# Slots without loops, GpSimd's row sums ahead of its transfers, and ScalarE's copies ahead of tests, in a graph attention and feed-forward kernel

## The reference

```python
def gnn(input1, input2, adj, a1, a2):          # input1 = layernorm(x)
    e = input1 @ a1 + (input2 @ a2).T          # 4096 x 4096
    e = where(e > 0, e, 0.2 * e)
    att = softmax(where(adj > 0, e, -9e15), axis=1)
    att = 0.1 * att * sum(adj, axis=1) + 0.9 * adj
    return att @ input2
x = x + gnn(layernorm(x), input2, adj, a1, a2)
x = x + layernorm(x) @ weight.T + bias
```

## Time and profile before

| | |
|---|---|
| median of 3 runs | 408.13 us (406.33 to 408.9) |
| profiled execution, own time | 405.57 us |
| its span, first to last instruction | 403.7 us |
| mean granted TensorE clock | 0.989 |
| PE, DVE, ACT, POOL busy | 91%, 77%, 62%, 38% |

### The profile page before, as it was taken

One profiled execution on the slowest core, in us unless ns is written; L12 is line 12 of the kernel. 1 busy time (PEld: TensorE's weight loads), 2 busy tenths in 40 slices (PEclk: granted clock), 3 DMA queues, 4 the chain that ended last, 5 costly groups with the idle time before them and its releaser, 6 DMA issues.

```text
span 403.7 us, 9169 instructions
## 1 busy us (share of the span) xinstructions
PE 368.8 (91%) x3237; PEld 319.9 (79%) x3237; DVE 311.4 (77%) x790; ACT 251.2 (62%) x638; POOL 152.0 (38%) x255
## 2 busy tenths in 40 slices
PE   0579999879999999999999599999999999999992
PEld 0368878678888888888888488888888888888881
DVE  3989788899796886959595764968869595968873
ACT  2499998787676492919376094764929293765100
POOL 1787051735353624243353503536341331500101
PEclk9999999999999999999999899999999999999997
DMA  6999996938565629091835608357290000000000
GB/s 208 253 213 215 219 180 117 202 69 182 110 141 108 140 60 190 29 190 48 154 82 119 134 15 164 71 103 145 55 196 26 15 15 2 13 3 15 13 2 29
DMA packets 17358, 42.84 MB, mean 106 GB/s; under 512 B 1936, under 2 KB 8608, under 8 KB 17312
## 3 DMA queue, kind: packets, MB, share of 16 engines
q0 software_dynamic: 9216, 33.56, 43.1%
q1 hardware_dynamic: 8096, 8.67, 6.8%
HBM read 73.66 MB, written 2.11 MB: 188 GB/s over the span
## 4 chain that ended last, share of the span: by engine, by line
PE 76%; ACT 11%; DVE 6%; issue 3%; DMA 2%; POOL 1%; SPq 0%; POOLq 0%; DVEq 0%; ACTq 0%
PE acc_u L598 25%; PE acc_v L598 25%; PE acc_y L598 22%; ACT steep L453 6%; ACT minus L506 2%; PE small L592 2%; DMA plus<-in 2%; PE small L578 1%; DVE plus L879 1%; DVE plus L756 1%; ACT weights_u L492 1%; PE turned L567 1%; ACT weights_v L498 1%; DVE minus L759 1%; POOL adj_all L339 0%
## 5 line engine op out<-in xcount | busy, mean ns | idle before, releaser
L453 ACT ACTIVATE steep<-s_bc,steep_s 128x256 bf16<-128x256 f32 x512 | 208.0, 496 | 11.5 <-DVE plus L756 11.4
L598 PE MATMUL acc_u<-weights_u,plus 128*128 128x258 f16 x1024 | 122.1, 275 | 5.6 <-issue 4.2
L598 PE MATMUL acc_y<-weights_y,adj_all 128*128 128x258 f16 x1024 | 121.1, 275 | 3.0 <-DVE lin L777 2.5
L598 PE MATMUL acc_v<-weights_v,minus 128*128 128x258 f16 x1024 | 120.3, 273 | 0.0
L598 PEld LDWEIGHTS acc_u<-weights_u,plus 128*128 128x128 bf16 x1024 | 100.3, 98 | 22.0 <-issue 4.8
L598 PEld LDWEIGHTS acc_y<-weights_y,adj_all 128*128 128x128 bf16 x1024 | 100.2, 98 | 18.7 <-DVE lin L777 2.8
L598 PEld LDWEIGHTS acc_v<-weights_v,minus 128*128 128x128 bf16 x1024 | 99.9, 98 | 14.4
L466 ACT ACTIVATE num<-acc_u,ac 128x129 f32<-128x129 f32 x32 | 11.5, 363 | 113.7 <-PE acc_u L598 113.7
L759 DVE TENSOR_TENSOR minus<-adj_all,plus 128x2048 bf16<-128x2048 bf16 x64 | 78.4, 1225 | 2.2
L756 DVE TENSOR_TENSOR plus<-adj_all,steep 128x2048 bf16<-128x2048 bf16 x64 | 78.5, 1226 | 0.9 <-ACT steep L453 0.9
L339 POOL DMA_DIRECT2D adj_all<-adj x64 | 36.0, 580 | 106.0 <-DVE minus L759 97.4
(11 more groups left out here) (78 smaller groups left out, 242.3 us busy)
## 6 DMA issues: line engine op xcount, KB each, us to landing
adj_all<-adj POOLq DMA_DIRECT2D x64, 512.0 KB, 8.9
plus<-in SPq DMA_DIRECT2D x4, 512.0 KB, 7.2
x_pre<-x SPq DMA_DIRECT2D x16, 128.0 KB, 2.1
x_res<-x SPq DMA_DIRECT2D x16, 128.0 KB, 2.2
out<-late SPq DMA_DIRECT2D x16, 128.0 KB, 5.2
s_rows<-s_bc SPq DMA_DIRECT2D x16, 1.0 KB
steep<-a SPq DMA_DIRECT2D x1, 64.0 KB, 3.1
a_bc<-a SPq DMA_DIRECT2D x1, 64.0 KB, 5.0
```

The costliest lines, as they stand in the source:

```text
L453: ins = nc.scalar.activation(steep[:, h, k, :], s1_bc[b][:, :], ACT.Relu, bias=steep_s2[:, jt:jt + 1], scale=STEEP)
L598: ins = nc.tensor.matmul(acc[:, 0:2 * WC], left[:, jt, cols(t)], right[:, jt, :, :].rearrange("p a b -> p (a b)"), start=(jt == 0), stop=( ...
```

## The change

Three things. First, `run_slots` no longer makes a loop: all 16 slots are written out on ACT, PE and DVE, and with n always a plain number the waits' values are constants. Second, POOL's slot has a new order. Third, ACT's two copies become a step that stands in a list: in slot 1 they are before quarters 2 and 3 of the tests, in the other slots at the end as they were.

```diff
-        def run_slots(eng, slot):
-            for c in range(BUFS):
-                slot(c, c)
-            with eng.Fori(1, CHUNKS // BUFS - 1) as quad:
-                for k in range(BUFS):
-                    slot(BUFS * quad + k, k)
-            for c in range(CHUNKS - BUFS, CHUNKS):
+        def run_slots(slot):
+            for c in range(CHUNKS):
                 slot(c, c % BUFS)
         def landed(n, b):
-            return 16 * (n // 2 + 1) if isinstance(n, int) else 8 * (n - b) + 16
+            return 16 * (n // 2 + 1)
...
             for c in range(CHUNKS):
                 b = c % 2
+                if c >= 1:
+                    post(c - 1, 1 - b)
+                if c + 2 < CHUNKS:
+                    row_sums(c + 2, b)
                 if c + BUFS < CHUNKS:
                     pool.wait_ge(y_done, 2 * c + 2)
                     pool.wait_ge(minus_ready, 4 * c + 4)
                     load_adj(c + BUFS)
-                if c >= 1:
-                    post(c - 1, 1 - b)
                 if c + 2 < CHUNKS:
-                    row_sums(c + 2, b)
                     factors(c + 2, b, False)
...
-                order = [0, 1, "first", "second", 2, 3] if isinstance(c, int) and c < 2 else \
-                    [0, 1, "first", 2, 3, "second"]
+                order = [0, 1, "first", "second", 2, 3, "copies"] if c == 0 else \
+                    [0, 1, "first", "second", "copies", 2, 3] if c == 1 else \
+                    [0, 1, "first", 2, 3, "second", "copies"]
                 for step in order:
-                    if step == "first":
+                    if step == "copies":
+                        if ahead(c, 2):
+                            copy_spread(c + 2, b)
+                        if inner(c):
+                            copy_turned(c - 1)
+                    elif step == "first":
                         numerator(c, 0, b)
...
-                if ahead(c, 2):
-                    copy_spread(c + 2, b)
-                if inner(c):
-                    copy_turned(c - 1)
-            run_slots(act, slot)
+            run_slots(slot)
```

More of the change, by code:

```diff
@@ L229, in cols @@
             return slice(tile * P, (tile + 1) * P)
-        def run_slots(eng, slot):
-            for c in range(BUFS):
-                slot(c, c)
-            with eng.Fori(1, CHUNKS // BUFS - 1) as quad:
-                for k in range(BUFS):
-                    slot(BUFS * quad + k, k)
-            for c in range(CHUNKS - BUFS, CHUNKS):
+        def run_slots(slot):
+            for c in range(CHUNKS):
                 slot(c, c % BUFS)
         def landed(n, b):
-            return 16 * (n // 2 + 1) if isinstance(n, int) else 8 * (n - b) + 16
+            return 16 * (n // 2 + 1)
         def adj_in(n, f):
-            return 16 * (n // BUFS + 1) if isinstance(n, int) else 4 * (n - f) + 16
+            return 16 * (n // BUFS + 1)
         def inner(c):
-            return not isinstance(c, int) or c >= 1
+            return c >= 1
         def ahead(c, k):
-            return not isinstance(c, int) or c + k < CHUNKS
+            return c + k < CHUNKS
         def wait_apart(eng, signal, value):
@@ L352, in row_sums @@
                 pool.wait_ge(pre_scaled, n + 1)
-                if not isinstance(n, int) or n >= 2:
+                if n >= 2:
                     pool.wait_ge(ac_ready, n - 1)
@@ L448, in sign_tests @@
                 h = q % 2
-                if q >= 2 or not isinstance(n, int) or n >= 1:
+                if q >= 2 or n >= 1:
                     act.wait_ge(plus_ready, 4 * n + q - 1)
@@ L572, in spread @@
                 pe.wait_ge(pre_pool, PRE * n + 3)
-                if not isinstance(n, int) or n >= 1:
+                if n >= 1:
                     pe.wait_ge(s1_ready, n)
-                if not isinstance(n, int) or n >= 4:
+                if n >= 4:
                     pe.wait_ge(out_ready, n - 3)
@@ L583, in linear @@
                 pe.wait_ge(xnt_ready, n + 1)
-                pe.wait_ge(s1_ready, n + 4 if not isinstance(n, int) else min(n + 4, CHUNKS))
+                pe.wait_ge(s1_ready, min(n + 4, CHUNKS))
                 if inner(n):
                     pe.wait_ge(out_ready, n)
-                if isinstance(n, int) and n == RANGE_AT:
+                if n == RANGE_AT:
                     pe.wait_ge(range_step, 5)
@@ L676, in slot @@
                     return
-                if isinstance(c, int) and c == 1:
+                if c == 1:
                     for q in range(QUARTERS):
@@ L696, in slot @@
                     y_product(c + 2, 1, (f + 2) % BUFS)
-            run_slots(pe, slot)
+            run_slots(slot)
             turn(CHUNKS - 1)
@@ L834, in finish @@
                 dve.wait_ge(x1b_ready, n + 1)
-                if not isinstance(n, int) or n >= 2:
-                    dve.wait_ge(out_stored[b], 16 * (n // 2) if isinstance(n, int) else 8 * (n - b))
-                if isinstance(n, int) and n == RANGE_AT:
+                if n >= 2:
+                    dve.wait_ge(out_stored[b], 16 * (n // 2))
+                if n == RANGE_AT:
                     dve.wait_ge(outside_summed, 1)
@@ L958, in slot @@
                             linear_part(c + 1, t, 1 - b)
-                    if not isinstance(c, int) or c >= 2:
+                    if c >= 2:
                         finish(c - 2, b)
@@ L963, in slot @@
                     pre_start(c + 2, b)
-                if isinstance(c, int) and c == CHUNKS - 1:
+                if c == CHUNKS - 1:
                     for q in range(QUARTERS):
@@ L969, in slot @@
                     dve.wait_ge(v_low, QUARTERS)
-                order = [0, "first", "second", 1, 2, 3] if isinstance(c, int) and c == 0 else \
+                order = [0, "first", "second", 1, 2, 3] if c == 0 else \
                     [0, 1, "first", 2, 3, "second"]
@@ L982, in slot @@
                     finish(c - 1, 1 - b)
-            run_slots(dve, slot)
+            run_slots(slot)
             last = CHUNKS - 1
```

## The result

The median fell from 408.02 us (406.33 to 408.9) to 395.62 us (395.23 to 395.78): ratio 0.9699, 95% interval 0.9667 to 0.9732, with four runs of each kernel. The profiled execution took 395.78 us, its span is 394.0.

The account below looks back on a forecast made before the run. PE, busy 368.8 of 403.7 us, was taken as nearly the bound. Savings of 6.0 and 3.9 us gave a 393.8 us span, 395.7 for the execution, and with 2.3 carried over 398.0 us; range 394.3 to 402.4.

Parts of the forecast that it names:

- The loop: PE's backward jump at slot 8: removing it saves 4.18 us of gap and 1.81 of lower clock, 6.0 in all.
- Rival (a): Straight code on PE has its own exposed fetches, 6.0 us each; 2 in 100 for over 412.2 us.
- Rival (c): Only the early part pays, the 4.18 us at slot 8 being something else than the jump: 404.0 us, 5 in 100.
- POOL and ACT in slot 1: New orders in slot 1: PE's waits for pre_s and late go, saving 1.18 + 2.76 = 3.9 us.
- The term of 3.9: Slot 2 on PE begins at 83.1 instead of 87.05; 3.9 us saved, bounds 1.5 and 4.1.
- Slacks: Margins before PE would wait: plus of quarter 3 2.2 us, pre_s of chunk 4 about 1.4, slot 2's copies 2.
- Rival (b): Only the loop pays, another wait replacing the two early ones: 400.4 to 401.9 us, 14 in 100.
- the other end: POOL's pre_s of chunk 3 stretched by 1.67 us beside DVE's masks, costing PE 0.2 us; zero was taken.
- The transfers, "zero": POOL issues each chunk's transfers later, by about 11 us in slot 8: no loss, and a gain excluded.
- The sum: 6.0 + 3.9 = 9.9 us off the 403.7 us span: 393.8, with 1.87 around it 395.7 us.
- Cases d: The forecast itself, whole kernel at 396 to 399.5 us: 79 in 100.
- 0.94: Chance that the whole kernel is faster by over 1%, under 404.05 us.

Follow-up runs that it names:

- experiment 2: Two kernels moving only slot 8's burst of adj transfers: one_burst_moved against the kernel before, 403.41 us; one_burst_back against loops_kept, 402.28 us.
- unroll_only: The kernel before with all slots written out on ACT, PE and DVE, old orders of POOL and ACT kept: 400.50 us, ratio 0.984.
- bodies_long: The changed kernel with three added two-turn PE loops, bodies of 1600, 1728 and 1984 instructions, at slots 4, 8 and 12: 993.39 us, one execution.
- one_burst_moved: The kernel before, but in slot 8 alone POOL issues chunk 12's transfers behind row_sums(10), not ahead of post(7): 403.41 us, ratio 0.989.
- loops_kept: The kernel before with the new orders of POOL and ACT, the loop on ACT, PE and DVE kept: 397.60 us, ratio 0.976.
- one_burst_back: loops_kept, but in slot 8 alone POOL issues its four transfers ahead of post(7) again: 402.28 us, 4.7 over loops_kept.
- hole_filled: unroll_only with 24 extra matmuls on PE in slot 1 ahead of linear(0), where PE waited for ACT's late: 399.91 us.

## Why the prediction was right

**The loop.** 6.0 us with the jump named as the cause: right in place, cause and size for this pair of kernels, though the size is not the jump's own: 1.6 us are, and the other 4.4 come of the burst under way (experiment 2). Rival (a), straight code with exposed fetches, didn't occur: PE's row has no gap after slot 2. Rival (c) fell with unroll_only. What the Trainium skill says (Runtime: NRT & Kernel Launch, Instruction fetch mechanics), that a taken branch to a page that isn't held forces a fetch, agrees with the packets: 8 in the second turn of the old loop. The section's window of two pages doesn't agree: the 1600 instructions of a body in bodies_long were still held on PE, with 1 packet in the second turn, and the measurement decides.

**POOL and ACT in slot 1.** Forecast and measured: DVE's late at 69.5 and 69.55, spread at 74.48 and 74.46, tests 2 at 75.9 and 75.64, slot 2 at 83.1 and 82.88. The term of 3.9 measured 4.2. The small differences come from counting turn at 0.76 us, which without a wait takes 0.66, and from small<-wt_sb, which without a wait is shorter by 0.1 too. Slacks: plus of quarter 3 was done at 82.24 + 1.23 = 83.5 (83.6 forecast); pre_s of chunk 4 ended at 92.23 and PE took it at 93.45, slack 1.2 (1.4 forecast); the copies of slot 2 ended at 99.6, and PE's next small stood at 101.26, slack 1.7 (2 forecast). Rival (b) needed one of these to be overdrawn; none was. pre_s of chunk 3 took 0.54 us beside DVE's first mask (72.52, against 71.75), not the 2.2 of the other end. The old rows had said so already: pre_s ran for 0.54 us at 75.07 beside a mask of 74.30 to 75.55, so pre_h's 2.21 was no measure of a mask's presence. The contention that the Trainium skill tells of (GPSIMD Engine Reference, Key points) cost PE nothing here.

**The transfers, "zero".** For the changed kernel this is right: in slot 8 the burst starts at 222.57, 4.2 us behind PE's 218.32, as foreseen, and nothing waits for it. As a term it was mis-stated: I said that nothing gains from later transfers, yet with the loop in place moving them in one slot was worth 4.5 us (one_burst_moved) and 4.7 (loops_kept against one_burst_back). It didn't show in the sum because the unrolling removes the jump with which the burst collided. The terms don't add: 10.3 and 7.4 apart, 12.4 together.

**From the profile to the median.** The sum gave 395.7 us for an execution like the profiled one, and the profiled one took 395.78. I then added 2.3 for the distance between the old profile and the old median. This is the step that was off, by those 2.3 us. The profiled execution of before was the fastest of all its runs, without the fall of the clock behind the hole. That most others had it is inferred, not traced: their mean clock is 0.979 to 0.988 against 0.989, and the hole cost a part of the runs of unroll_only 1.7 us. The change closes the hole, so most of the distance went with it. That the sum met the profiled execution within 0.1 us is partly luck: the early term was 0.3 us too small, and the 0.5 us of the tail were not in it. I had named the jump as the possible source of the scatter; hole_filled shows the hole to be one, and one_burst_back, with the jump at its full price and the hole gone, has runs within 0.7 us. Of the 12.4 us, 4.2 and 6.0 are in the two traces, less 0.5 of the tail, and some 1.7 the hole's clock; about 1 us of the old median is not traced to anything.

**The chances.** Cases d and b and half of c add up to 95.5 in 100, where I wrote 0.94. Nothing hangs on it.

## What to carry to other kernels

Look at where the bound engine stands for "issue" at a loop's end: here a long loop was fetched anew at its jump, where loops of up to 1600 instructions were not, and the packet that PE waited for started 2.5 us later when a burst of data was under way, so the price depended on what another engine had just issued. Before adding up the parts of a change, ask whether one of them removes the place where another one pays. A median that lies above the profiled execution is a term too: compare the clock of the runs, and look for a hole on PE behind which it falls in some of them. If runs of one kernel lie at two levels, one profile shows only one of them.

## What the runs showed of the hardware

- A loop body of 1600 instructions on PE (800 matmuls and 800 weight loads) ran its second turn with no gap; bodies of 1728 and 1984, and the old loop (1620 by its source), stood for 1.36 to 1.62 us at the jump on quiet DMA engines, and the old loop for 4.1 to 4.2 us inside a burst of POOL's transfers. The long bodies ran in one execution each.
- PE went on 2.7 us after the start of a packet on the queue "instruction" at the old loop's jump, in four traces, with and without a burst; the burst moved the packet's start from 1.1 us ahead of the gap to 1.4 to 1.5 us into it.
- The clock fell behind the 4.1 us gap in both traces that have one (5.4 us for a group of 3.6), behind the 2.60 us hole in some executions only (one of four traces that have it), and in no trace behind the jumps of 1.36 to 1.62 us.
- POOL's pre_h, 128x2, took 2.21 us directly behind pre_s, and takes 0.35 where the transfers stand between (75.26 above), though DVE runs its masks in both. POOL's busy time fell from 152.0 to 129.3 us, with no effect on the end. In the old trace the row ends with one of DVE's masks; I haven't tested more.
